# First projection of a row and column attention: where two transposes of the row softmax stand, and who normalises the third tile

## The reference

```
Ks = n @ Wk_s, Qs = (row 0 of n) @ Wq_s      # per column c
sw = softmax over r of (Qs . Ks) / sqrt(16)  # row weights: (r, c, head)
Q  = (n @ Wq) * scaling * sw ; K = n @ Wk ; V = n @ Wv
attn = softmax over j of  sum over r, d of Q[r, i] . K[r, j]     # 192 x 192 per head
out  = x + sum over j of attn[i, j] V[r, j]
```

## Time and profile before

| | |
|---|---|
| three runs | 554.79, 559.97, 561.93 us; median 559.97 |
| profiled execution | span 562.5 us; its time is not listed apart from the span |
| TensorE busy | 521.5 us, 93% of the span |
| VectorE, ScalarE, GpSimd busy | 384.7, 284.4, 183.5 us (68, 51, 33%) |
| first projection | from about 85 to 285 us of the span |
| granted TensorE clock, mean | 0.960 of full speed |

### The profile page before, as it was taken

The page is one execution under the profiler, slowest core; times in us unless marked ns, Lnnn a source line. Parts: engine busy times, 40 slices in busy tenths (PEclk is TensorE's granted clock), DMA queues, the critical chain, the costliest instruction groups (busy, mean ns, idle before and its releaser), DMA issues.

```text
span 562.5 us, 16012 instructions
## 1 busy us (share of the span) xinstructions
PE 521.5 (93%) x6319; PEld 398.7 (71%) x6319; DVE 384.7 (68%) x1022; ACT 284.4 (51%) x601; POOL 183.5 (33%) x232
## 2 busy tenths in 40 slices
PE   7798698699999999999989999997899979999995
PEld 6697564255545555554579998897799979998884
DVE  2669958578877787778756678665366663667763
ACT  4456947687999999997522220004266551221000
POOL 3000214745777777776310000004255650000000
PEclk9778979799999999999999999999799999999998
DMA  8999012445566666689898999999979738997997
GB/s 327 384 332 381 24 56 106 154 138 167 197 208 216 206 195 219 202 211 213 161 228 250 295 308 364 298 342 272 345 269 333 254 99 244 299 318 266 237 236 206
DMA packets 186271, 134.44 MB, mean 239 GB/s; under 512 B 168992, under 2 KB 170848, under 8 KB 186208
## 3 DMA queue, kind: packets, MB, share of 16 engines
q1 hardware_dynamic: 153664, 120.88, 69.2%
q10 hardware_dynamic: 32544, 12.68, 9.3%
HBM read 76.92 MB, written 56.62 MB: 237 GB/s over the span
## 4 chain that ended last, share of the span: by engine, by line
PE 82%; DVE 8%; DMA 5%; ACT 1%; POOL 1%; issue 1%; SPq 0%; DVEq 0%; POOLq 0%; ACTq 0%
PE PS L1187 26%; PE PS L1195 14%; PE PS L1281 10%; PE PS L1285 6%; DVE EXTRA L770 5%; DMA EXTRA<-in_x 4%; PE PS L1316 3%; PE PS L1317 3%; PE PS L1320 3%; PE PS L1318 3%; PE PS L1319 3%; PE PS L1071 1%; PE PS L1148 1%; DMA EXTRA<-xt_scratch 1%; PE PS L1176 1%; PE PS L1088 1%
## 5 line engine op out<-in xcount | busy, mean ns | idle before, releaser
L1187 PE MATMUL PS<-WP,EXTRA 128*128 128x384 f16 (+1 forms) x1152 | 159.2, 290 | 5.5 <-DMA EXTRA<-xt_scratch 5.5
L1187 PEld LDWEIGHTS PS<-WP,EXTRA 128*128 128x128 f16 x1152 | 99.1, 99 | 52.4 <-issue 24.1
L492 POOL TENSOR_TENSOR EXTRA<-BIG,EXTRA 128x512 f16<-128x512 f32 x69 | 81.9, 1188 | 38.2 <-ACT EXTRA L592 29.9
L1195 PE MATMUL PS<-WP,EXTRA 64*128 64x384 f16 (+1 forms) x1152 | 90.6, 288 | 0.2 <-DVE EXTRA L909 0.2
L527 POOL TENSOR_TENSOR BIG<-EXTRA,BIG 128x384 f32 x48 | 43.8, 915 | 132.5 <-ACT BIG L712 129.1
L498 POOL TENSOR_TENSOR BIG<-EXTRA,BIG 128x192 f16<-128x192 f32 x96 | 53.8, 561 | 47.7 <-ACT BIG L650 47.7
L1195 PEld LDWEIGHTS PS<-WP,EXTRA 64*128 64x128 f16 x1152 | 44.3, 95 | 29.4 <-issue 18.4
L719 ACT CAST BIG<-PS 128x384 f32 (+1 forms) x48 | 23.1, 481 | 77.6 <-PE PS L1195 68.6
L1281 PE MATMUL PS<-BIG,EXTRA 128*128 128x128 f16 x960 | 62.0, 220 | 0.3
L899 DVE CAST BIG<-PS 128x192 f16<-128x192 f32 x96 | 34.3, 357 | 34.9 <-ACT EXTRA L643 34.3
L770 DVE BATCH_NORM_STATS2 EXTRA<-BIG 128x6 f32<-128x512 f32 x72 | 43.7, 678 | 20.3 <-ACT BIG L541 20.3
(11 more groups left out here) (178 smaller groups left out, 945.3 us busy)
## 6 DMA issues: line engine op xcount, KB each, us to landing
EXTRA<-in_x SPq DMA_DIRECT2D x24, 768.0 KB, 8.0
xt_scratch<-EXTRA SPq DMA_DIRECT2D x24, 768.0 KB, 3.4
BIG<-v_scratch SPq DMA_DIRECT2D x48, 384.0 KB, 5.2
EXTRA<-xt_scratch SPq DMA_DIRECT2D x24, 768.0 KB, 5.9
v_scratch<-EXTRA SPq DMA_DIRECT2D x32, 384.0 KB, 3.9
EXTRA<-in_x SPq DMA_DIRECT2D x24, 384.0 KB, 4.8
BIG<-in_x SPq DMA_DIRECT2D x24, 384.0 KB, 6.7
out_x<-BIG ACTq DMA_DIRECT2D x18, 384.0 KB, 6.0
```

What stands on the lines that cost most here:

```text
L492: pool.tensor_tensor(tt[:, t, 1, :].rearrange("p (q n) -> p q n", n=P), raw(c, t), tt[:, t, 0, :].rearrange("p (q n) -> p q n", n=P), ALU. ...
L1187: ins = mm(outs[a], xt[:, t, s, q * P:(q + 1) * P], WP[:, t, w, wc], start=first and j == 0, stop=last and j == 2, skip_group_check=True)
L1195: ins = mm(outs[a], xt[rows, 1, s, q * P:(q + 1) * P], WP[rows, 1, w, wc], start=first and j == 0, stop=last and j == 2, skip_group_check= ...
```

## The change

Four lists are reordered, and one tile in three changes its engine.

- TensorE: scores_transposed(c+1) moves from between groups 0 and 1 to between groups 1 and 2, ahead of scores(c+2); weights_back(c+1) moves from between groups 2 and 3 to behind group 3. Both then stand between full-height parts.
- VectorE: the maximum of chunk c+1 moves behind group 1, the reciprocal behind group 2; from chunk 5 on VectorE normalises the third tile, behind group 0.
- ScalarE: the exponent moves behind the q copy of group 0 (ahead of the V copy of group 2), normalise_weights behind the q copy of group 1 (ahead of the V copy of group 3), row_weights behind the V copy of group 3; the third tile's normalising is left out.
- The counts that xn_high waits for follow the new owner of the tile.

```
 def xn_high(c):                                   # ScalarE
-        act.wait_ge(s_n, 6 if c == 3 else 3 * (c - 2))
+        act.wait_ge(s_n, 6 + 2 * max(c - 4, 0))
+        if c > 4:
+            act.wait_ge(s_nd, 9 + c - 4)
...
 # ScalarE, loop over c
     q_high0(c - 1, NQ - 1)
-    if c + 1 < NCH:
-        exponent(c + 1)
     if c + 4 < NCH:
         normalise_x(c + 4, (0,))
     v_high0(c, 1)
+    q_high0(c, 0)
     if c + 1 < NCH:
-        normalise_weights(c + 1)
-    q_high0(c, 0)
+        exponent(c + 1)
     if c + 2 < NCH:
         scores_low(c + 2)
-    if c + 4 < NCH:
-        normalise_x(c + 4, (1,))
     v_high0(c, 2)
     q_high0(c, 1)
     if c + 1 < NCH:
+        normalise_weights(c + 1)
+    if c + 4 < NCH:
+        normalise_x(c + 4, (1,))
+    v_high0(c, 3)
+    if c + 1 < NCH:
         row_weights(c + 1)
-    if c + 4 < NCH:
-        normalise_x(c + 4, (2,))
-    v_high0(c, 3)
...
 # VectorE, loop over c
-    if c + 1 < NCH and c > 1:
-        score_max(c + 1)
     for g in range(NQ):
         k_high0(c, g)
         weighted_q(c, g)
         kv_low0(c, g)
         if c == 1 and g == 0:
             score(2)
-            score_max(2)
-        if g == 0 and c + 1 < NCH:
-            invert_sums(c + 1)
         if g == 0 and vectors:
             queries_by_head((c + 1) // 2)
+        if g == 0 and c + 4 < NCH:
+            normalise_x(c + 4, (2,))
+        if g == 1 and c + 1 < NCH:
+            score_max(c + 1)
         if g == 1 and c + 2 < NCH:
             score(c + 2)
+        if g == 2 and c + 1 < NCH:
+            invert_sums(c + 1)
...
 # TensorE, loop over c, behind project0(c, 0)
     if c == 1:
         scores(2)
         weights_back(1)
-    elif c + 1 < NCH:
+    project0(c, 1)
+    if c + 1 < NCH:
         scores_transposed(c + 1)
-    project0(c, 1)
-    if c == 1:
-        scores_transposed(2)
     if c + 2 < NCH:
         scores(c + 2)
     project0(c, 2)
+    project0(c, 3)
     if c + 1 < NCH:
         weights_back(c + 1)
-    project0(c, 3)
```

More of the change, by code:

```diff
@@ L214, in row_column_attention @@
         s_n = sem("xnT_ready")
-        s_nd = sem("xnT_ready_chunks_1_2_4")
+        s_nd = sem("xnT_ready_by_vector")
         s_h = sem("xnT_highs")
```

## The result

The changed kernel takes 621.48 us (617.47 to 623.73), the kernel before 560.95 in the same comparison: ratio 1.111, 95% interval 1.105 to 1.118. The forecast was 610 us, range 598 to 624. Medians, here and in the table of experiments, are of all executions of a kernel; ratios leave out executions in a slower state of the chip and are taken against the kernel before as it ran beside each kernel.

What follows compares the result with a forecast made beforehand. TensorE was taken to set the pace before, at 7.57 us a chunk, and ScalarE and VectorE taking turns after; 562.5 us profiled plus 42.7 for the turn and 7 for the clock gave 612, 610 against the median, range 598 to 624.

Steps and rivals of the forecast that it cites:

- The turn of ScalarE and VectorE: First projection: ScalarE's waits for maximum and reciprocal make both engines alternate; chunk at least 9.75 us, 2.18 over the present.
- The x tile on VectorE: Third x tile behind VectorE's group 0, a link of the chunk's cycle: taken as 0.66 us, 0.45 at the short end.
- The clock: TensorE's clock falls after its gap in 12 of 18 steady chunks, making the V copy 0.6 us late: 7 us.
- The gap and the clock: TensorE idles 2.74 us per chunk in front of weights_back; similar gaps before suggested a clock fall in two of three chunks.
- the first rival: The turn of the two engines happens but TensorE's clock holds: 603 us; chance 0.22.
- The transposes: Moved between TensorE's full groups, each costs 0.07 us instead of 0.35; TensorE needs 7.01 us per chunk, from 7.57.
- The last chunks: Chunks 20 to 22, without x tiles: the turn runs over TensorE, 8.44 us each, some 3 us more for the three.
- Chunks 2 and 3: Counted among chunks 2 to 19 at 2.18 us each; chunks 1 and 3, with new score vectors, add some 0.5.
- The step from the profile to the median: The profiled execution, 562.5 us, was taken as 2.5 us above the median of the runs, turning 612 into 610.
- falls in each chunk (635): Rival: TensorE's clock falls in each chunk through both groups, 1.8 us each: 635 us; chance 0.08.
- That TensorE stays the bound (548): Rival: VectorE delivers maximum and sums before ScalarE asks, 22 chunks gain 0.56 us: 548 us; chance 0.03.
- That the change does nothing (556 to 560): Rival: a transpose drains as much between full groups and the softmax hides too: 556 to 560 us; chance 0.03.

Runs made afterwards that it cites:

- e8: Changed kernel with only VectorE's maximum moved ahead of its group 1, the reciprocal left behind group 2; 601.86 us, 1.077 of the kernel before.
- e9: Changed kernel with only VectorE's reciprocal moved ahead of its group 2, the maximum left behind group 1; 593.47 us, 1.062 of the kernel before.
- e2: Changed kernel with VectorE's maximum ahead of its group 1 and its reciprocal ahead of its group 2; 572.49 us, 1.030 of the kernel before.
- e6: As e4, but VectorE normalises the third x tile one chunk earlier (chunk c+5's in chunk c); 553.50 us, 0.984 of the kernel before.
- e4: As e2, and VectorE's third x tile moved behind group 3; 576.99 us, 1.030 of the kernel before.
- e1: Changed kernel with the third x tile put back on ScalarE, behind the second one; 611.07 us, 1.097 of the kernel before.
- e5: Kernel before with only the third x tile moved to VectorE, behind group 0 from chunk 5 on; 559.91 us, 1.002 of the kernel before.

## Why the prediction was right, point by point

- **The turn of ScalarE and VectorE: right, and shown.** Both waits stand where they were put, 2.67 us (forecast 2.1) and 1.23 us (forecast 1.3). e8, e9 and e2 remove them one by one and together, and each chunk length, where chunks repeat, agrees within 0.1 us with the sum that has the tile at its measured length.
- **The x tile on VectorE: the mis-sized term.** The prediction had bounds of 0.45 and 0.66 us, from the rows of tiles that ran beside the end of a subtraction of GpSimd or beside none; it measured 1.39 in the steady chunk. That alone turns 9.75 into 10.48 us; over 18 chunks it is 13 us. I named GpSimd's subtraction beside it and then took the longest row that I had as its price. No row of before has a tile that starts together with a 128x512 subtraction, but the trace of before held the size: the 0.73 us tile of the earlier trace rows began 0.88 us into a subtraction and ended 0.28 us after it. The changed kernel has the same end, whether the tile starts with the subtraction (209.60 above) or later. The subtraction of before, and then tile and subtraction of a later chunk (timelines of GpSimd and VectorE):

```profile
89.03 1.33 POOL L492 TENSOR_TENSOR EXTRA<-BIG,EXTRA 128x512 f16<-128x512 f32 x1
```

```profile
231.05 1.01 DVE L837 TENSOR_SCALAR BIG<-BIG,small 128x512 f32<-128x512 f32 x1
```

```profile
230.61 1.16 POOL L492 TENSOR_TENSOR EXTRA<-BIG,EXTRA 128x512 f16<-128x512 f32 x1
```

  In e4 the same instruction stands where GpSimd waits, and takes 0.54 us instead of the 1.47 of e2. That agrees in kind with the Trainium skill (GPSIMD Engine Reference, section Specifications), by which two-port operations of VectorE contend with GpSimd for SBUF; the section gives no size.
- **The clock: right that it falls, wrong where it costs.** It was given 7 us, for falls in 12 of the 18 steady chunks. Of the 15 steps from the exponent of chunk 4 to that of chunk 19 it falls in 6 (granted clock 0.84, once 0.70; 1.00 in the others), and 13 steps take 10.49 us all the same. The two others took 10.80 and 11.43 us, 1.3 us more in all. The longer tile gave TensorE 0.7 us more lead; and where the V copy of group 0 came late in spite of it, three times by 0.5 to 0.8 us, the tile began later beside the same subtraction and took 0.98 to 1.01 us instead of 1.47, as in the lines above. The clock costs more in chunk 3, whose score vectors took 7.4 us (134.79 to 142.18), against 4.15 for the same ones before (130.87 to 135.02), at this clock:

```profile
130.00:140.00 10.00, 7.22 (x29) 3.72 (x24) 5.12 (x18) 3.87 (x11) 1.58 (x2) 0.72 0.43 143
```

- **The gap and the clock.** In the steady chunks of the changed kernel the gap is 3.20 us where TensorE lost nothing in the chunk ahead; after two of these (at 163.20 and 173.69) the clock stayed at 1.00. e1 has a gap near the forecast's 2.74, 2.58 us, and there the clock did fall in some chunks. TensorE's timeline, behind weights_back (L1178), in a chunk with the fall and in the next without:

```profile
201.29 0.30 PE L1178 MATMUL PS<-ident,EXTRA 96*128 96x96 f32 x1 [2.58 <-ACT EXTRA L630]
201.43 1.77 PE L1184 MATMUL PS<-WP,EXTRA 128*128 128x384 f16 x6
...
211.52 0.30 PE L1178 MATMUL PS<-ident,EXTRA 96*128 96x96 f32 x1 [1.35 <-ACT EXTRA L630]
211.66 1.14 PE L1184 MATMUL PS<-WP,EXTRA 128*128 128x384 f16 x6
```

  The Trainium skill (TensorE: Matmul & The Clock Gate, section Why this matters for your kernels) warns only of gaps longer than the one forecast. That a shorter gap leaves the clock alone, as the first rival took from it, e1 does not bear out; the measurement decides.
- **The transposes: right.** Two half-height groups in a row, and a transpose between full groups nearly free: 0.50 us a chunk in e6. In the changed kernel it shows only as a longer gap.
- **The last chunks: right.** From the exponent of chunk 20 to 21 and 22 it takes 8.65 us each (318.45, 327.10, 335.75); the sum over TensorE gave 8.44. The step into chunk 20, behind the last x tile, still takes 10.23.
- **The whole, and some luck.** The stage grew by 64.4 us: 45.7 between the exponents of chunks 4 and 19 (forecast 15 x 2.18 = 33, and 11 for the tile's true size), 10.5 from the exponent of chunk 2 to that of chunk 4, 3.6 behind that of chunk 19, 4.6 ahead of that of chunk 2 (4.0 of these only because the exponent now stands later in its chunk). Chunks 2 and 3 are the second mis-sized term: the forecast gave them 2 x 2.18 = 4.4 us and a share of 0.5. Part of the 10.5 is the low clock over the score vectors; the rest was not taken apart. So 621 lies in the range partly by luck: its upper end, 624, stood for 21.6 us of clock falls in the steady chunks, of which the trace has 1.3, and the tile and chunks 2 and 3 filled that room. The step from the profile to the median was off as well: in every other run here the time is 1.7 or 1.8 us longer than the span, so the profiled execution of before lay some 4.3 us above the median, not 2.5, which would have made the forecast 608.
- **Rivals.** That the clock holds everywhere (603) or falls in each chunk (635): neither. That TensorE stays the bound (548) is ruled out in this kernel, whose gap is 3.20 us, and becomes true in e6. That the change does nothing (556 to 560) is ruled out by the ratio of 1.111.

## What to carry to other kernels

In lists that run in order, judge a small step's place by how long ago the thing it waits for became ready. If it has to wait for a whole group of another engine, a step of 0.3 us couples the two engines, and the links of that cycle add up, however idle both look. Before moving a step, write down for both engines what is queued behind it, close the loop, and sum it. With the tile's true length the sum here was good to 0.1 us, save in e4, where a reader had been left out of it. Then let the step's producer run ahead of the bulk work, and place work that is only needed later with its next reader in view (e4 and e6 differ by one chunk and 23 us). And price each link in the company that it will have: beside GpSimd's subtraction the tile took 1.39 us, not 0.66.

## What the runs showed of the hardware that was not expected

A VectorE tensor_scalar of 128x512 fp32, SBUF to SBUF, took 0.54 us alone and 1.39 to 1.48 us when a GpSimd tensor_tensor of 128x512 began within 0.05 us of it; GpSimd's instruction kept its 1.16 us. Where it began 0.44 us into the subtraction it took 1.01 us, and in the traces of before, of the changed kernel and of e5 it ended 0.27 to 0.29 us after the subtraction. So it looks as if the VectorE instruction stood until GpSimd's was through; that is read from the timelines, and was not tried with other sizes. When the granted clock of TensorE fell in 6 of 15 chunks, four of these still took 10.49 us, since another cycle held them.
